# Keys and queries of a cross-attention transposed by their projections and stacked by transfers, score matmuls over 96 rows

## The reference

```python
q = layernorm(x) @ Wq + bq                 # 256 x 256 a batch
k = concat([x2 @ Wk + bk, memory])         # 512 keys: 256 projected, 256 from memory
v = concat([x2 @ Wv + bv, memory])
attn = softmax(q k^T * 16**-0.5)           # for each of 16 heads
x = x + (attn @ v) @ Wp + bp
z = layernorm(x)
cw = softmax(z @ w_router) * softmax(z @ w_gating / 0.1), normalised
x = x + sum over experts of cw * ((silu(z @ w_gate) * (z @ w_up)) @ w_down)
```

## Time and profile before

| what | value |
|---|---|
| median of three runs | 2773.96 us (2772.17 to 2774.82) |
| the profiled execution's own time | 2771.69 us |
| its span | 2769.6 us |
| granted TensorE clock, mean | 0.994 of full |
| busy: TensorE, VectorE, ScalarE, GpSimd | 98%, 73%, 61%, 62% |
| transfers | 252 MB, 91 GB/s over the span |

### The profile page before, as it was taken

The page is one execution under the profiler, slowest core; times in us unless marked ns, Lnnn a source line. Parts: engine busy times, 40 slices in busy tenths (PEclk is TensorE's granted clock), DMA queues, the critical chain, the costliest instruction groups (busy, mean ns, idle before and its releaser), DMA issues.

```text
span 2769.6 us, 48148 instructions
## 1 busy us (share of the span) xinstructions
PE 2721.2 (98%) x16465; PEld 2228.0 (80%) x16465; DVE 2009.8 (73%) x3254; ACT 1689.5 (61%) x3241; POOL 1720.9 (62%) x1886
## 2 busy tenths in 40 slices
PE   7789999999999999999999999999999999999998
PEld 5568888888888888888888888888888888888887
DVE  6877777768777777777777778677776867665554
ACT  7766666666666666565666666666666665544443
POOL 6766566666666566666665666665665665654554
PEclk9999999999999999999999999999999999999999
DMA  2113233332333322333232322323323233333332
GB/s 69 40 54 101 76 99 96 92 101 79 99 93 93 102 84 88 96 95 100 83 95 83 106 89 85 103 81 109 94 80 101 78 99 92 93 107 116 104 104 83
DMA packets 251280, 252.32 MB, mean 91 GB/s; under 512 B 15904, under 2 KB 242848, under 8 KB 251040
## 3 DMA queue, kind: packets, MB, share of 16 engines
q1 hardware_dynamic: 251040, 249.25, 29.6%
HBM read 240.66 MB, written 8.52 MB: 90 GB/s over the span
## 4 chain that ended last, share of the span: by engine, by line
PE 92%; issue 3%; DVE 2%; ACT 2%; POOL 1%; DMA 0%; SPq 0%; POOLq 0%; ACTq 0%; DVEq 0%
PE ps_t L670 25%; PE ps_o L704 24%; PE ps_s L670 24%; PE ps_s L764 4%; PE ps_t L774 4%; PE ps_m L549 3%; PE ps_a L746 2%; PE ps_a L748 2%; PE ps_m L607 1%; PE ps_m L567 1%; PE ps_m L622 1%; PE ps_m L614 1%; ACT Pt L928 0%; DVE Pt_lo L1154 0%; DVE negmax L1146 0%
## 5 line engine op out<-in xcount | busy, mean ns | idle before, releaser
L949 DVE SCALAR_TENSOR_TENSOR hf<-hf,ps_s 128x512 f32<-128x512 f32 x512 | 350.2, 684 | 401.5 <-ACT hf L788 400.3
L794 ACT ACTIVATE h_hi<-ps_t 128x512 fp32r<-128x512 f32 x512 | 306.2, 598 | 451.1 <-DVE ps_t L956 451.1
L961 DVE TENSOR_TENSOR h_lo<-ps_t,h_hi 128x512 fp32r<-128x512 f32 x512 | 353.0, 689 | 213.9 <-ACT h_hi L794 207.6
L788 ACT ACTIVATE hf<-ps_s 128x512 f32<-128x512 f32 x512 | 306.3, 598 | 329.8 <-PE ps_s L670 327.7
L1185 POOL TENSOR_TENSOR wg_lo<-stage_w,wg_hi 128x512 fp32r<-128x512 f32 x256 | 337.4, 1318 | 265.5 <-ACT wg_hi L801 264.7
L1250 POOL TENSOR_TENSOR Pt_lo<-Pt 128x512 f16<-128x512 f32 x256 | 289.7, 1132 | 197.9 <-ACT Pt L928 197.0
L704 PE MATMUL ps_o<-h_lo,wd_hi 128*128 128x512 f32 x1024 | 399.9, 390 | 0.0
L704 PE MATMUL ps_o<-h_hi,wd_hi 128*128 128x512 f32 x1024 | 398.5, 389 | 0.9 <-DVE h_lo L961 0.9
L704 PE MATMUL ps_o<-h_hi,wd_lo 128*128 128x512 f32 x1024 | 398.4, 389 | 0.0
L956 DVE TENSOR_TENSOR ps_t<-hf,ps_t 128x512 f32<-128x512 f32 x512 | 356.4, 696 | 48.1 <-PE ps_t L670 7.5
L1185 POOL TENSOR_TENSOR wd_lo<-stage_w,wd_hi 128x512 fp32r<-128x512 f32 x256 | 332.1, 1297 | 87.5 <-ACT wd_hi L801 87.5
(11 more groups left out here) (192 smaller groups left out, 5092.4 us busy)
## 6 DMA issues: line engine op xcount, KB each, us to landing
stage_w<-in_L_ffn_w_gate_dram SPq DMA_DIRECT2D x256, 256.0 KB, 2.7
stage_w<-in_L_ffn_w_up_dram SPq DMA_DIRECT2D x256, 256.0 KB, 3.0
stage_w<-in_L_ffn_w_down_dram SPq DMA_DIRECT2D x256, 256.0 KB, 2.7
cwb<-d_cw SPq DMA_DIRECT2D x64, 256.0 KB, 3.6
X<-in_x_dram SPq DMA_DIRECT2D x32, 256.0 KB, 3.2
C<-in_fside_BxSxS_dram SPq DMA_DIRECT2D x16, 256.0 KB, 3.0
KVM<-in_ctx_dram SPq DMA_DIRECT2D x16, 256.0 KB, 2.8
d_x<-X SPq DMA_DIRECT2D x16, 256.0 KB, 2.9
```

What stands on the lines that cost most here:

```text
L788: act.activation(hf[:], ps_g[:], ACT.Tanh, scale=0.5).then_inc(tanh_done, 1)
L794: act.activation(h_hi[f % FC][:], ps_u[:], ACT.Copy).then_inc(hh_done, 1)
L949: dve.scalar_tensor_tensor(out=hf[:], in0=hf[:], scalar=1.0, in1=ps_g[:], op0=ALU.add, op1=ALU.mult).then_inc(gate_done, 1)
L961: dve.tensor_tensor(h_lo[f % FC][:], ps_u[:], h_hi[f % FC][:].bitcast(F32), ALU.subtract).then_inc(hl_done, 1)
```

## The change

Keys and queries are projected with the weights as the stationary operand, so that they come out transposed (features in the rows). ScalarE adds the bias and writes the high part, VectorE the low part. The sync engine stores both parts in device memory (`d_k`, `d_q`) and loads them back three times into row blocks of `KTs` and `QTs`, 32 rows to a block (16 for each of two heads): high, low, high for keys and high, high, low for queries, each for four pairs at a time. Rows 96 to 127 hold the ones (keys) and the maxima (queries). The score matmul of L764 contracts over the first 96 rows only, so maxima left by the batch before don't matter; L774's contracts over all 128. The stacks, the items kT and the query half of qq are gone; kv becomes k and v, the memory's keys are transposed by a new item m. `QTs` holds all eight pairs. The scale is put into Wq. The keep-busy transposes go from 49 to 65. VectorE makes `low_part` and `router_weights` ahead of the item as long as no expert work runs.

```diff
-    HS = SLOTS * HD
+    HS = 2 * ROWS
+    TOP = 3 * ROWS
+    GP = PAIRS // 2
...
+    d_k = nc.dram_tensor("d_k", [B, 2, D, NK], F32, kind="Internal").ap()
+    d_q = nc.dram_tensor("d_q", [B, 2, D, N], F32, kind="Internal").ap()
...
-        qstack = sb("qstack", [P, QT * H, SLOTS, HD], F32R)
-        kstack = sb("kstack", [P, KC * H, SLOTS, HD], F32R)
-        QTs = sb("QTs", [P, QRING, 2, N], F32R)
+        qT_hi, qT_lo = sb("qT_hi", [P, DC, N], F32R), sb("qT_lo", [P, DC, N], F32R)
+        kT_hi, kT_lo = sb("kT_hi", [P, DC, NK], F32R), sb("kT_lo", [P, DC, NK], F32R)
+        QTs = sb("QTs", [P, PAIRS, 2, N], F32R)
+        key_rows = sb("key_rows", [P, NK])
...
+        ITEMS = [(1, "cT", 0, 1), (2, "qm", 1, 0), (4, "k", 0, 1), (5, "aT", 0, -1), (6, "qm", 2, 0), (8, "o", 0, -1),
+                 (9, "v", 0, 1), (10, "qm", 3, 0), (11, "xT", 0, 1), (12, "m", 0, 1), (13, "q", 0, 1), (14, "qm", 4, 0),
+                 (15, "x2T", 0, -1), (17, "lg", 0, -1), (18, "qm", 5, 0), (21, "y", 0, 0), (22, "qm", 6, 0),
+                 (23, "cwT", 0, -1), (24, "y", 1, 0), (26, "qm", 7, 0), (30, "qm", 0, 1)]
+
+        FIRST_AT = {"cT": (1,), "xT": (2,), "k": (4,), "m": (6,), "q": (7,), "v": (9,)}
...
+                eng.wait_ge(const_ready, CONSTS)
+                eng.dma_start(KTs[TOP:P].bitcast(F32), key_rows[TOP:P].unsqueeze(1).broadcast_to([ROWS, PAIRS, NK])).then_inc(rows_in, 16)
+
+            def store_keys(turn, d):
+
+                turn.wait(eng, k_l, d, 2)
+                turn.wait(eng, m_l, d, 1)
+                for n, part in enumerate((kT_hi, kT_lo)):
+                    eng.dma_start(d_k[turn.b + d, n].rearrange("(c p) n -> p c n", p=P), part[:].bitcast(F32)).then_inc(k_out.sem, 16)
...
+            def place_keys(turn, d, g):
+
+                turn.wait(eng, k_out, d, 32)
+                turn.wait(eng, t_ps, d - 1, 2 * OCT * (g + 1))
+                for slot, part in enumerate((0, 1, 0)):
+                    eng.dma_start(KTs[slot * ROWS:(slot + 1) * ROWS, g * GP:(g + 1) * GP, :].bitcast(F32),
+                                  d_k[turn.b + d, part, bass.ds(g * P, P)].rearrange("(a r) n -> r a n", r=ROWS)).then_inc(k_in[g].sem, 16)
+
+            def place_queries(turn, d, g):
+
+                turn.wait(eng, q_out, d, 32)
+                turn.wait(eng, t_ps, d - 1, 2 * OCT * (g + 1))
...
+                for slot, part in enumerate((0, 0, 1)):
+                    src = d_q[turn.b + d, part, bass.ds(g * P, P)].rearrange("(a h r) n -> h r a n", h=2, r=HD)
+                    for h in range(2):
+                        r = slot * ROWS + h * HD
+                        eng.dma_start(QTs[r:r + HD, pairs, h, :].bitcast(F32), src[h]).then_inc(q_in[g].sem, 16)
...
+                    first = turn.b == -1
+                    if turn.has(1) and step == (10 if first else 14):
+                        store_keys(turn, 1)
+                    if turn.has(1) and step == (10 if first else 15):
+                        store_queries(turn, 1)
+                    if turn.has(1) and step == (11 if first else 17):
+                        place_keys(turn, 1, 0)
+                    if turn.has(1) and step == (11 if first else 19):
+                        place_queries(turn, 1, 0)
+                    if turn.has(0) and step == 1:
+                        place_keys(turn, 0, 1)
+                    if turn.has(0) and step == 3:
+                        place_queries(turn, 0, 1)
...
-            KEEP_BUSY = {(-2, 0): 13, (-1, 2): 10, (-1, 4): 6, (-1, 19): 10, (-1, 22): 2, (-1, 24): 8}
+            KEEP_BUSY = {(-2, 0): 13, (-1, 2): 10, (-1, 4): 6, (-1, 24): 36}
...
+                    if name in ("k", "q"):
+                        full, hi, out_c, b_at, used = {"k": (k_ps, kT_hi, k_h, 1, k_out), "q": (q_ps, qT_hi, q_h, 0, q_out)}[name]
...
+                        for m in range(DC):
+                            act.activation(hi[:, m, 0:N], ps[:, m * N:(m + 1) * N], ACT.Identity,
+                                           bias=bT[:, b_at, m:m + 1]).then_inc(out_c.sem, 1)
...
+                            act.activation(QTs[TOP:TOP + 3, k, h, :], ps[HS * h + ROWS:HS * h + ROWS + 3, 0:N],
+                                           ACT.Copy).then_inc(qm_done.sem, 1)
...
-                        pe.matmul(score_bank(j)[:], QTs[:, h // 2 % QRING, h % 2, qt * P:(qt + 1) * P],
-                                  KTs[:, h // 2, :], start=True, stop=True).then_inc(s_ps.sem, 1)
+                        pe.matmul(score_bank(j)[:], QTs[0:TOP, h // 2, h % 2, qt * P:(qt + 1) * P],
+                                  KTs[0:TOP, h // 2, :], start=True, stop=True).then_inc(s_ps.sem, 1)
...
-            pool.memset(qstack[:, :, 2, :].bitcast(F32), 0.0).then_inc(const_ready, 1)
+            pool.memset(key_rows[:], 0.0).then_inc(rows_clear, 1)
+            pool.memset(QTs[:].bitcast(F32), 0.0).then_inc(const_ready, 1)
```

More of the change, by code:

```diff
@@ L569, in transpose_in, with project_across @@
                 return mm
-            def stack_block(stack, t, pair):
-                return stack[:, t * H + 2 * pair:t * H + 2 * pair + 2].rearrange("p h s d -> p (h s d)")
+            def project_across(ps, col, a, w):
+                (act, act_lo), (wt, wt_lo) = a, w
+                for m in range(DC):
+                    n, last = 0, 3 * DC - 1
+                    for tok, half in ((act, wt), (act, wt_lo), (act_lo, wt)):
+                        for c in range(DC):
+                            mm = pe.matmul(ps[:, m * N:(m + 1) * N], half[:, c, col + m * P:col + (m + 1) * P], tok[:, c, :],
+                                           start=(n == 0), stop=(n == last))
+                            n += 1
+                return mm
             def do_misc(turn, name, k, d, one, freed):
@@ new lines, in body @@
+                    if name == "m":
+                        turn.wait(act, m_ps, 1, 1)
+                        turn.wait(act, k_out, 0, 32)
+                        act.activation(kT_hi[:, :, N:NK], ps[:].rearrange("p (c n) -> p c n", n=N), ACT.Copy).then_inc(m_h.sem, 1)
+                    if name == "qm":
+                        turn.wait(act, qm_ps, d, k + 1)
+                        for h in range(2):
+                            act.activation(QTs[TOP:TOP + 3, k, h, :], ps[HS * h + ROWS:HS * h + ROWS + 3, 0:N],
+                                           ACT.Copy).then_inc(qm_done.sem, 1)
@@ L1031, in router_weights, with low_part @@
                                       ALU.mult).then_inc(cw_done.sem, 1)
+            def low_part(turn, step):
+                d, i = item_at(step, -1)
+                if turn.has(d) and by_dve(i):
+                    turn.wait(dve, exp_done, d, i + 1)
+                    slot = i % RING
+                    dve.tensor_tensor(Pt_lo[slot][:], Pt[slot][:], Pt[slot][:].bitcast(BF16)[:, 1::2],
+                                      ALU.subtract).then_inc(lo_dve.sem, 1)
             def normalise(turn, d, src, m, r, dst, done):
@@ L1147, in body @@
                                           negate=True).then_inc(max_done.sem, 1)
[L1149 to L1155 removed]
+                    if f is not None:
+                        router_weights(turn, step)
+                        low_part(turn, step)
             turns(body)
```

253 lines of the change are left out of this document (99 added, 154 removed), and 4 rows, old and new, of the table ITEMS.

## The result

The changed kernel takes 2711.97 us (median of four runs, 2709.15 to 2714.3) against 2774.36 us (median of four, 2772.17 to 2774.82) before: ratio 0.9775, 95% interval 0.9764 to 0.9787, 62 us less. The prediction was 2725, 2702 to 2758. The profiled execution took 2711.55 us, its span is 2709.8 against 2769.6.

What follows compares the result with a forecast made beforehand. TensorE, busy 98% of the span, was taken as the bound, with no engine full before the first expert matmul. The terms -56.1 + 5.3 + 1.2 - 4.2 + 3 - 8 + 10 gave -48.8 us: 2725 us, range 2702 to 2758.

Steps and rivals of the forecast that it cites:

- After the cut: From the first expert matmul to the end, TensorE almost always busy: every TensorE instruction removed wins time, predicted -50.8 us.
- kT: TensorE's item of four key transposes: 104 removed after the first expert matmul at 0.36 us each, -37.4 us.
- wait of step 20: TensorE's up projection waiting for h_lo, 0.32 us once a batch, taken as gone with the stack copies: -4.2 us.
- new waits for h_lo: After the first expert matmul, VectorE's four added half-width subtractions delay h_lo: +3 us, bounds 0 and 12.
- The score matmuls: Score matmuls over 96 rows stream the same 512 columns on TensorE: no cost taken, upper bound 0.16 us each way.
- Transfers: After the first expert matmul, 63 MB more on the sync queue, covered by slack of the weight loads: no cost.
- Rival C: Narrow loads so slow that weights come late, from 7 us a burst: 2746 or 2811; chance 0.04 plus 0.03.
- Before the cut: Attention alone, 143 us until the first expert matmul: 8 us won, bounds 20 won and 12 lost.
- VectorE loses nothing: In the attention-only stretch VectorE, fullest with 118 of 143 us, loses no work and gets about 1 us a turn.
- Rival A: More won before the first expert matmul, the round following VectorE: 20 instead of 8, start 7, total 2710; chance 0.12.
- Rival B: Trips through device memory late before the first expert matmul: start 16, 12 lost instead of 8 won, 2751; chance 0.15.
- The start: Keys and queries travel out and back before the first score: first transposed scores 10 us later, bounds 5 and 16.

Runs made afterwards that it cites:

- a_burst7: The changed kernel with each key burst raised from 0.79 to 1.84 MB by four more loads into a tile nobody reads: 2716.32 us.
- b_qs21: The kernel before with ScalarE's query stack copy and GpSimd's subtraction behind it moved from step 18 to 21: 2770.56 us.
- a_clear2: a_warm with GpSimd's clearing of QTs moved from the front to just behind VectorE's XN operations: 2706.74 us.
- a_warm: Changed kernel, first three weight loads moved to turn 0, rows of ones written by GpSimd, 100 keep-busy transposes instead of 36 before the first score: 2707.58 us.

## Why the prediction was right, and where its sizes were off
The sign and the mechanism of the long part held: after the cut the kernel is TensorE's instructions in a row. Step by step:

**After the cut: forecast -50.8 us, measured -56.8.** From the starts of transposed score matmuls, averaged by step over turns 3 to 14, the turn fell from 168.34 to 163.83 us.

| term | predicted | measured a turn or item | over the run |
|---|---|---|---|
| kT | -37.4 | 0.385 each, 104 of them (0.36 predicted) | -40.0 |
| query transposes | -18.7 | 1.41 a turn in the eight steps, less 0.14 that is a wait | -16.5 |
| m | +5.3 | 0.50 x 12 | +6.0 |
| k, v and q for kv, kv and q | +1.2 | 0.05 x 12 | +0.6 |
| wait of step 20 | -4.2 | 0.41 x 13 (0.32 predicted) | -5.3 |
| wait of step 22 | not seen | 0.14 x 13 | -1.8 |
| new waits for h_lo | +3 | none | 0 |

That sums to -57.0, but the closeness to -56.8 is in part luck. In the twelve turns averaged the terms make 52.2 us and 54.1 were measured; 1.9 us lie in small changes of other items (steps 5, 8, 15, 21 and 23) that no term has. Outside those turns the terms make 4.8 and 2.8 was measured. The forecast of the counted instructions, -49.6 against -49.9 by the table, is so close because two errors cancel: kT took 2.6 us more out than forecast and the query transposes 2.2 less. Two other terms were mis-sized. The removed wait was read off one turn; it is larger on average and has a second place, step 22, which the row of one step could not show. And the 3 us of new waits didn't come. The waits of TensorE after the cut show it, the kernel before first, then after (us in total, times, longest):
```profile
PE ps_t L670 <- DVE h_lo L961: 2.6, 14, 0.5
```
```profile
PE ps_t L706 <- DVE h_lo L981: 1.2, 3, 0.9
```
14 such waits of the up projection have become 3: VectorE's four added subtractions fit. The view gives the waits of before 2.6 us in all, the step averages 0.55 a turn, some 7 us in 13 turns: it counts only the time after the matmul before has ended, 0.15 us in the earlier trace rows, where the starts lie 0.32 further apart than their work. Starts are what the end of the run sees.

**The score matmuls: nothing, right.** The Trainium skill speaks on both sides. By "TensorE: Matmul & The Clock Gate", "LDWEIGHTS (loading the stationary operand)", the time of a weight load goes with its columns and not with its rows, and this case's traces agree, 0.46 us for the pair with 96 and 0.47 with 128 rows. By "TensorEngine Tiling (Array Packing)", "Key Properties", a change of tiling mode drains the array; whether 96 of 128 rows is such a change the Trainium skill doesn't say there. No drain shows at 96 rows between 128-row neighbours, and the medians are 0.2 us apart.

**Transfers: nothing, right, with an error in the rate.** The added 63.2 MB kept the engines busy for 39.0% of 2709.8 less 29.6% of 2769.6 us, 237 us: 267 GB/s, where 304 was taken and half of it was the other bound. In a key burst the engines are full (share, then GB/s, as the last two numbers of each row of after):
```profile
1225.00:1228.00 3.00, 3.00 (x17) 2.48 (x16) 2.07 (x4) 1.62 (x3) 1.29 (x1) 1.00 0.99 238
1228.00:1231.00 3.00, 3.00 (x15) 2.47 (x14) 2.29 (x5) 1.70 (x4) 0.96 (x1) 1.00 0.98 219
```
In this stretch lie the three key loads of a burst (0.79 MB into 32 partitions) and two loads of 0.26 MB into 128, so the rates are of the mixture. By landings alone, the third key load of a burst lands 2.3 us after the first (median of 32 bursts), with 0.52 MB in between: 228 GB/s. That is three quarters of 304, not half. By "SBUF — State Buffer", "Door 1: The DMA port swizzle", the Trainium skill gives 32 partitions 8 of 16 ports and with them about 218 GB/s, and the trace lies at that figure or up to a tenth above it. So that figure of the Trainium skill is borne out; what does not hold is the prediction's halving of 304, since the wider loads ran well below the 436 GB/s that it gives for 16 ports. For 16 partitions nothing is shown: the query loads are 64 KB each and six take 2.72 us to issue, 145 GB/s, so they did not fill the engines. Rival C falls, and a_burst7 shows that it would have needed bursts of over twice the size.

**Before the cut: forecast -8 us, measured -16.1 and -11.5.** The mechanism was half right. Giving the copies back costs 3.4 to 5.4 us, so ScalarE's relief is real, but it is the smaller part. The step that failed is "VectorE loses nothing": the order in which it works was not priced at all, and that was worth 6 to 8 us in the changed kernel. The two together are 9.5 to 13.5 us, about what was measured; they need not add, and what the items gone from TensorE and its waits for L916 bring there was not measured by itself. The differences of single traces are rough besides: this stretch takes 126.4 to 131.8 us in nine executions of the new order, and 142.65 and 145.38 in before and b_qs21, which differ there only in the step of one copy and its subtraction. Rival A named the outcome, a round near VectorE's work (121 of 126.5 us busy), for a reason that holds only in part. Rival B fell: behind the first score TensorE waits once in the stretch for queries, 0.8 us, and never for keys. (The prediction's 39 us of ScalarE in 32 steps is 42 by the earlier trace rows, 110 us over 2.6 turns; nothing hangs on it.)

**The start: forecast +10 us, measured +13.1 and +12.0.** Some 1.5 us of the excess of 2.0 to 3.1 is XN's delay behind the held-up tensor_scalar, if it passes on in full; in a_clear2 XN came 0.70 us earlier than in a_warm and the first score 1.13. The prediction knew the clearing only as a possible late QTs. The rest, 0.5 to 1.6 us, was not taken apart; it lies within the bounds of 5 to 16. That transfers set this time was right: 2.4 to 5.1 us went with the three weight loads. The timeline of the sync queue after shows the two trips, stores at 13.85 and 16.84, loads issued at 24.21 and 25.58, the second half from 28.35. The second key store landed at 24.19, 9.9 us after its issue, and the first load went out right behind it:
```profile
13.85 0.37 SPq L439 DMA_DIRECT2D d_k<-kT_hi  x1
...
24.21 1.28 SPq L452 DMA_DIRECT2D KTs<-d_k  x3
25.58 2.72 SPq L466 DMA_DIRECT2D QTs<-d_q  x6
28.35 1.37 SPq L452 DMA_DIRECT2D KTs<-d_k  x3
```

Together, by the first execution: 3.1 us more at the start, 8.1 more won before the cut, 6.0 more after it, 11 us in all, which is the span's 2709.8 against 2720.8. 2712 is the lower edge of the forecast's own range (2712 to 2740) and lies nearer to the 2710 of rival A, though not by A's start of 7 us, which was 12 to 13. The errors stay small beside the forecast because its largest terms, 56.1 us out and 6.5 in, rested on instructions counted and priced by differences of starts.

## What to carry to other kernels
Where one engine has no gaps, price each of its instructions by the difference of starts with and without it, and average over all turns rather than read one; the counted instructions were 50 of the 60 us here, forecast within 1 us in sum. Where no engine is full, look at the order of work inside each engine before the amount: moving two calls ahead of others won 6 to 8 us, where ScalarE's relief of a fifth (110 to 85 us in that stretch) won 3 to 5. Do not judge such a stretch by one trace: compare its granted clock and its length over several executions first. Put a long memset of GpSimd where VectorE has no tensor_scalar to do.

## What the runs showed of the hardware that was not expected
- A memset by GpSimd holds up a tensor_scalar of VectorE until it ends: 7.28 instead of 0.73 us under two memsets of 3.5 us, 1.72 instead of 0.17 under the rest of a row of them, 0.69 instead of 0.17 in a_clear2. All of these are float32 from SBUF to SBUF. tensor_tensor and scalar_tensor_tensor beside the same memset kept their 0.68 us, two scalar_tensor_tensors in a row their 1.28. A memset of GpSimd takes 3.51 to 3.54 us for 4096 columns, on 3, 32 or 128 partitions alike.
- Loads into 32 partitions with rows of 2 KB ran at 228 GB/s by their landings, and at 219 to 238 mixed with loads into 128 partitions with the transfer engines full, against the 304 GB/s of the kernel before.
- A stretch in which engines wait for each other differs by 4.6 us between two executions of one kernel (126.55 and 131.13), with VectorE's busy time the same and the granted TensorE clock at 0.92 and 0.84. The 2543 us in which TensorE has no gaps differ by 0.2 between these two, and lie between 2541.4 and 2543.6 in eight with the same program there.
